# Turn, mix and projection of a node tile in one iteration of the chunk loop, with a written-out end for each convolution

## The chip, the cores and the metric

The kernel runs on one core of one Trainium2 chip. The metric is the device time of one execution in microseconds (us). Before the change it is 4954.78 us, the median of three runs (4953.78 to 4971.25).

## What is computed

A graph network on 12,500 nodes of 256 features and 200,000 edges sorted by destination. First `h = relu(layernorm(x))`, then two graph convolutions with self loops, then a projection, added to x:

```
h = h @ W_pre + b_pre
h = relu(gcn(h, W1, b1)); h = relu(gcn(h, W2, b2))
x = x + h @ W_post + b_post
gcn: out[d] = sum over edges (s, d) of (h @ W)[s] * dinv[s] * dinv[d]; out + b
```

Then a second layer: `h = relu(layernorm(x))`, `xt = h @ weight`, four attention heads whose logits come from the rows of the two ends of an edge, a softmax over the heads, and a weighted sum of the heads, which is added to x. Only the first n = 12,500 edges are used for it.

## The kernel before, in words

Nodes lie in 98 tiles (TILES) of 128 rows. Edges lie in 1568 chunks of 128, eight chunks to a half, two halves to an iteration, 98 iterations (ITERS) and 196 halves to a convolution. A convolution is c = 0 or c = 1.

**Gathers.** POOL (L631 to L637) issues one indirect DMA for each chunk: it fetches the table rows of the chunk's 128 sources into G. G has 12 portions (PORTIONS) of one half each, so before a half's first gather POOL waits until PE has finished the half 12 before it (`g_agg`, L635). The second convolution's first gather waits until the whole second table is in DRAM (`c1_w`, L630).

**Sums.** PE multiplies each chunk with a 0/1 selection matrix that DVE made (`chunk`, L959) and adds the eight products of a half in PSUM. Its last matmul signals `g_agg`. DVE adds the sum to one or two accumulator tiles (L1380), makes the selection for the half four later (`select`), and after an even half 2i makes the scaled rows of tile i-1 (`rows`, L1280, signal `c_tmp`). A matmul of f32 shows as two records in the profile: a chunk is x2.

**Work of a node tile, c = 0.** PE turns the rows (`turn`, L922), ACT copies them out (`lift`, L689), PE multiplies by Wc (`mix`, L931), ACT applies bias and relu (`relu_mixed`), PE multiplies by W2 (`project`, L942), ACT scales the result and writes it to `tsb` (`table_row`, L709), and SP stores it as a tile of the second table.

**Work of a node tile, c = 1.** `turn`, ACT's `relu_rows`, `project` by Wp; DVE's `residual` (L1291) adds x and takes mean and variance, with a square root on ACT in the middle; ACT's `normed` (L718) writes h; PE turns h (`turn_normed`, L949), ACT copies it (`normed_turned`), PE multiplies by Wx (`attention`, L954), ACT copies the result (`projected`, L730), and SP stores it to `xtab` and `ltab`. The attention stage, which follows, waits for all of these stores (L546, L613).

**The order.** Each engine runs its own list in order, written out by hand; waits for semaphores are the only tie. PE places the tile work between the chunks j = 0 to 15 of iteration i (L1000 to L1013). Before the change: for c = 0, `mix(i-3)` ahead of j = 2, `project(i-3)` ahead of j = 8, `turn(i-2)` ahead of j = 12; for c = 1, `turn_normed(i-4)` ahead of j = 2, `project(i-3)` ahead of j = 6, `attention(i-4)` ahead of j = 10, `turn(i-2)` ahead of j = 12. Four more passes of the loop without chunks finish the last tiles. ACT's list (L794 to L810) follows the same order. DVE runs `residual(i-3)` in iteration i (L1389 to L1393) and three residuals after the loop.

Of the kernel before, what the change touches and what calls it, by code (L numbers as in the profile page):

```python
# [29 lines left out]
CPH = CPG * HALF  # L30
# [15 lines left out]
def build_gnn(nc, x, src, dst, W_pre, b_pre, W1, b1, W2, b2, W_post, b_post, weight, attn_l,  # L46
# [5 lines left out]
    TILES = ceil(N, P)  # L52
    LAST = N - (TILES - 1) * P
    NP = TILES * P
    ITERS = ceil(E, CPI * P)
# [26 lines left out]
    with ExitStack() as ctx:  # L82
# [283 lines left out]
        def due(t):  # L366
            return 0 <= t < TILES
# [283 lines left out]
        def _(act):  # L651
            act.wait_ge(s_esrc, 16 * (1 + (FULL % P > 0) + (REST > 0)))
            act.copy(rawf_s, raw_s).then_inc(s_raws, 1)
            n = 0
# [34 lines left out]
            def lift(t):  # L689

                act.wait_ge(c_T, t + 3)
                act.copy(zc[:, :, :].rearrange("p k n -> p (k n)"), pT[0][:, 0:D])
                act.copy(sd_row, pT[0][0:1, D:D + P]).then_inc(c_l, 1)  # L693

            def relu_mixed(t):

                act.wait_ge(c_m, t + 1)
                act.wait_ge(c_a, t + 1)
                for m in range(KH):
                    ins = act.activation(z[:, m, :], pX[:, m * P:(m + 1) * P], ACT.Relu, bias=b1_c[:, m:m + 1])  # L700
                ins.then_inc(c_z, 1)
# [7 lines left out]
            def table_row(t):  # L709

                if isinstance(t, int):
                    act.wait_ge(c1_w[t % 2], 16 * (t // 2 + 1))
                else:
                    act.wait_ge(c1_w[0], t * 16 + 16)
                act.wait_ge(c_a, t + 2)
                act.activation(tsb[:, t % 2 if isinstance(t, int) else 0, :], pA[0][:, 0:D], ACT.Copy, scale=dinv[:, bass.ds(t, 1)]).then_inc(c_out, 1)
# [75 lines left out]
            bad = act.value_load(flag_i[0:1, 0:1], min_val=0, max_val=1)  # L792
            with act.If(bad == 0):
                for c in range(2):  # L794
                    for i in range(2, ITERS + 4):
                        if c == 0:
                            if due(i - 3):
                                relu_mixed(i - 3)
                                table_row(i - 3)
                            if due(i - 2):  # L800
                                lift(i - 2)
                        else:
                            if due(i - 4):
                                normed_turned(i - 4)
                            if due(i - 3):
                                normed(i - 3)
                            if due(i - 4):
                                projected(i - 4)
                            if due(i - 2):
                                relu_rows(i - 2)  # L810
                fast_attention()
            with act.Else():
                act.sem_inc(w_done, 1)
# [22 lines left out]
        def _(pe):  # L836
# [160 lines left out]
            with pe.If(bad == 0):  # L997
                for c in range(2):

                    for i in range(ITERS + 4):  # L1000
                        for j in range(CPI):
                            if j == 2 and c and due(i - 4):
                                turn_normed(i - 4)
                            if j == 2 and c == 0 and due(i - 3):
                                mix(i - 3)
                            if j == (6 if c else 8) and due(i - 3):
                                project(c, i - 3)
                            if j == 10 and c and due(i - 4):
                                attention(i - 4)
                            if j == 12 and due(i - 2):  # L1010
                                turn(c, i - 2, i % 2)
                            if i < ITERS:
                                chunk(c, 2 * i + j // CPH, j % CPH)  # L1013
                transpose_sel(0, 0, 0, True)
                for q in range(2):
                    pick(0, q, False)
                with pe.Fori(1, BATCHES // 2 - 1) as j:
                    for q in range(2):
                        pick(j, q, False)
                for q in range(2):  # L1020
                    pick(BATCHES // 2 - 1, q, True)
            with pe.Else():
                pe.wait_ge(s_din, 16)
                pe.transpose(pX[:, 0:TILES], degr, ident[0:TILES, 0:TILES]).then_inc(s_degT, 1)
                for c in range(2):
                    n = width(c)
# [17 lines left out]
        def _(dve):  # L1044
# [317 lines left out]
            with dve.If(bad == 0):  # L1362
                link(dve.tensor_copy(iota_p, iota[:, :]))
                link(dve.tensor_copy(bias_p, b2_bc[:, :]))
                for H in range(RING):
                    select(H)
                for c in range(2):
                    loaded, wide = 0, D if c else D + 1
                    for n in range(HALVES):
                        H = n + c * HALVES  # L1370
                        at = first_tile(n)
                        dve.wait_ge(g_agg, H + 1)
                        if H:
                            dve.wait_ge(g_add, 2 * H)
                        for a, mask in enumerate((here, beyond)):
                            T = at + a + c * TILES
                            if at + a >= loaded:
                                dve.wait_ge(a_in[T % AR], 16 * (T // AR + 1))
                                loaded += 1
                            dve.scalar_tensor_tensor(out=row(T, wide), in0=sums[H % SUMS][:, 0:wide],  # L1380
                                                     scalar=mask[:, n:n + 1], in1=row(T, wide),
                                                     op0=ALU.mult, op1=ALU.add).then_inc(g_add, 1)
                        if H + RING < 2 * HALVES:
                            select(H + RING)
                        if n % 2 == 0:
                            if due(n // 2 - 1) and n // 2 < TILES - 1:
                                dve.wait_ge(g_add, 2 * H + 2)
                                rows(c, n // 2 - 1, (n // 2 - 1) % 2, 1)
                            if c and due(n // 2 - 3):  # L1389
                                if n // 2 == 3:  # L1390
                                    for s in range(2):
                                        dve.wait_ge(c1_w[s], 16 * (TILES // 2 + 1))
                                residual(n // 2 - 3)  # L1393
                    dve.wait_ge(g_add, 2 * (c + 1) * HALVES)
                    for t in (TILES - 2, TILES - 1):
                        rows(c, t, t % 2, 1)
                    if c:
                        for t in range(TILES - 3, TILES):
                            residual(t)
                for q in range(2):  # L1400
                    select_f(q, q)
                dve.wait_ge(f_T, 2)
# [83 lines left out]
```

## Time and profile before

| | us |
|---|---|
| median of 3 runs | 4954.78 |
| profiled execution, its own time | 4990.98 |
| profiled execution, span | 4989.2 |
| first gather / last gather of c = 0 | 167.0 / 2399.6 |
| first gather / last gather of c = 1 | 2481.8 / 4712.5 |
| first gather of the attention stage | 4798.9 |

Busy shares of the span: PE 54%, POOL 62%, DVE 27%, ACT 9%. The mean granted clock of TensorE is 0.711 of full speed. The profile is one execution, 36.2 us longer than the median. In the timeline each row has its start, its length, engine, line, operation, output and inputs and, in brackets, how long the engine had been idle and what released it.

### The profile page before, as it was taken

How to read it: one execution, taken by the hardware profiler on the slowest of the kernel's cores; microseconds unless marked ns; L12 is line 12 of the kernel's file. 1: busy time of each engine (PE TensorE's matmuls, PEld its weight loads, DVE VectorE, ACT ScalarE, POOL GpSimd, SP SyncE). 2: the span in 40 equal slices, each digit the busy share in tenths (PEclk: the TensorE clock that was granted, in tenths of full speed). 3: DMA queues.
4: the chain of work that ended last, by engine and by line, in shares of the span. 5: the costliest groups of instructions: out<-in, count | busy, mean ns of one | idle time of the engine just before them, and what ended most of it. 6: DMA issues, size and time to landing. Idle time of an engine off the chain costs nothing.

```text
span 4989.2 us, 31799 instructions
## 1 busy us (share of the span) xinstructions
PE 2687.9 (54%) x10154; PEld 2099.1 (42%) x10154; DVE 1346.5 (27%) x2984; ACT 441.6 (9%) x1265; POOL 3096.6 (62%) x3240
## 2 busy tenths in 40 slices
PE   3325465555555655656634555555555555555675
PEld 2214344444444444445522444444434434444453
DVE  8201111112111211211202322332222323223357
ACT  2100000000000000000100000000000000000022
POOL 0566666666666666666275666666666666666535
PEclk5557776777777777767756777777777777777765
DMA  6433343433343433333133444444444444444336
GB/s 188 125 94 101 104 107 104 107 104 104 104 107 103 107 105 104 104 104 107 57 105 91 118 114 114 117 112 117 114 112 119 115 112 118 113 116 116 99 106 186
DMA packets 318169, 556.09 MB, mean 111 GB/s; under 512 B 79912, under 2 KB 217976, under 8 KB 318008
## 3 DMA queue, kind: packets, MB, share of 16 engines
q0 software_dynamic: 153184, 413.34, 31.4%
q1 hardware_dynamic: 164824, 140.76, 9.4%
q8 instruction: 82, 1.34, 0.1%
q14 instruction: 79, 0.65, 0.0%
HBM read 489.06 MB, written 64.78 MB: 111 GB/s over the span
## 4 chain that ended last, share of the span: by engine, by line
another core or an unknown queue 46%; issue 24%; PE 19%; DVE 6%; ACT 4%; DMA 1%; SPq 0%; POOL 0%; ACTq 0%; DVEq 0%; POOLq 0%
PE agg L968 7%; PE pD L968 4%; PE pA L846 2%; PE pX L938 2%; PE pX L939 2%; ACT xin L700 1%; DVE acc L1380 1%; PE pT L840 1%; DVE sel L1136 1%; DVE xin L1126 1%; DVE sel L1351 0%; ACT h L723 0%; ACT xin L707 0%; PE pA L994 0%
## 5 line engine op out<-in xcount | busy, mean ns | idle before, releaser
L608 POOL DMA_INDIRECT G<-tab,idx x3126 | 2970.1, 950 | 1734.9 <-issue 1069.7
L968 PE MATMUL agg<-G,sel 128*128 128x257 f32 (+1 forms) x4192 | 1253.0, 444 | 235.3 <-issue 203.9
L968 PEld LDWEIGHTS agg<-G,sel 128*128 128x128 f32 x4192 | 929.5, 228 | 428.5 <-issue 271.9
L1380 DVE SCALAR_TENSOR_TENSOR acc<-agg,here,acc 128x257 f32<-128x257 f32 (+1 forms) x262 | 127.0, 485 | 2353.9 <-remote 1879.7
L968 PE MATMUL pD<-G,sel 128*128 128x257 f32 (+1 forms) x2080 | 644.1, 455 | 85.0 <-issue 81.1
L968 PEld LDWEIGHTS pD<-G,sel 128*128 128x128 f32 x2080 | 475.3, 234 | 188.4 <-issue 104.8
L1276 DVE TENSOR_TENSOR sel<-rel,pA 128x1024 f32<-128x1024 f32 x392 | 474.5, 1211 | 0.0
L938 PE MATMUL pX<-xin,Wc 128*128 128x128 f32 x784 | 169.0, 349 | 488.1 <-ACT xin L693 402.2
L846 PE MATMUL pA<-W2s,xin 128*128 128x256 f32 x392 | 137.4, 484 | 416.0 <-ACT xin L700 212.9
L1380 DVE SCALAR_TENSOR_TENSOR acc<-pD,here,acc 128x257 f32<-128x257 f32 (+1 forms) x130 | 63.0, 485 | 1105.0 <-remote 818.4
L938 PEld LDWEIGHTS pX<-xin,Wc 128*128 128x128 f32 x784 | 132.5, 234 | 529.6 <-ACT xin L693 417.1
L846 PE MATMUL pX<-Wx,hT 128*128 128x264 f32 x392 | 140.4, 492 | 351.1 <-issue 258.1
L846 PEld LDWEIGHTS pA<-W2s,xin 128*128 128x128 f32 x392 | 90.3, 243 | 449.9 <-ACT xin L700 222.8
L846 PE MATMUL pA<-Wp,xin 128*128 128x256 f32 x392 | 144.5, 506 | 236.3 <-ACT xin L707 210.3
L846 PEld LDWEIGHTS pX<-Wx,hT 128*128 128x128 f32 x392 | 92.4, 245 | 380.3 <-issue 267.3
L840 PE MATMUL pT<-ident,h 128*128 128x128 f32 x196 | 55.6, 377 | 295.0 <-issue 246.5
L846 PEld LDWEIGHTS pA<-Wp,xin 128*128 128x128 f32 x392 | 97.1, 258 | 276.2 <-ACT xin L707 231.4
L608 POOL DMA_INDIRECT lg<-ltab,fst x98 | 118.6, 1210 | 133.5 <-DMA ltab<-xin 85.4
L840 PEld LDWEIGHTS pT<-ident,h 128*128 128x128 f32 x196 | 24.2, 173 | 337.1 <-issue 281.4
L700 ACT ACTIVATE xin<-pX,b_c 128x128 f32<-128x128 f32 x196 | 61.4, 364 | 886.4 <-remote 649.0
L1380 DVE SCALAR_TENSOR_TENSOR acc<-agg,beyond,acc 128x257 f32<-128x257 f32 (+1 forms) x262 | 124.8, 476 | 0.0
L939 PE MATMUL pX<-xin,bc_row 1*128 1x128 f32 x392 | 117.0, 386 | 0.0
(182 smaller groups left out, 1663.9 us busy)
## 6 DMA issues: line engine op xcount, KB each, us to landing
G<-tab,idx POOLq DMA_INDIRECT x3126
tab<-G SPq DMA_DIRECT2D x14, 910.0 KB, 5.1
acc<-tab SPq DMA_DIRECT2D x98, 130.0 KB
xtab<-xin SPq DMA_DIRECT2D x98, 130.0 KB
tab<-tsb SPq DMA_DIRECT2D x98, 128.0 KB
acc<-tab SPq DMA_DIRECT2D x98, 128.0 KB
xres<-acc SPq DMA_DIRECT2D x98, 128.0 KB
xin<-xres SPq DMA_DIRECT2D x14, 896.0 KB
```

The lines of the kernel that those rows point to most:

```text
L608: return pool.indirect_dma_start(out=to, out_offset=None, in_=table, in_offset=bass.IndirectOffsetOnAxis(ap=index, axis=0))
L700: ins = act.activation(z[:, m, :], pX[:, m * P:(m + 1) * P], ACT.Relu, bias=b1_c[:, m:m + 1])
L840: ins = pe.transpose(to[:, k * P:(k + 1) * P], of(k), ident[:, :])
L846: ins = pe.matmul(to[:, 0:n], lhsT(k), w[:, k, :], start=(k == 0), stop=(k == KH - 1))
L938: pe.matmul(to, Wc[:, k, m * P:(m + 1) * P], zc[:, k, :], start=(k == 0), stop=False)
L939: ins = pe.matmul(to, bc_row[0:1, m * P:(m + 1) * P], sd_row, start=False, stop=True)
L968: ins = pe.matmul(sums[H % SUMS][:, 0:n_c], sel[:, H % RING * CPH + j, :], G[:, H % PORTIONS * CPG + j, 0:n_c], start=(j == 0), stop=(j == ...
L1126: dve.tensor_tensor(ones_low[unit % BR][:, 0:n // 4, :, :], low_b[:, at:at + n].rearrange("p (q j) -> p q j", j=4).unsqueeze(2) .to_broadc ...
L1136: return dve.bn_stats(moms[:, m, :], xb[:, b % XB, m % FB, 0:D])
L1276: dve.tensor_tensor(sel[:, s * CPH:(s + 1) * CPH, :], rel[:, n * CPH:(n + 1) * CPH].unsqueeze(2).to_broadcast([P, CPH, P]), iota_p.unsquee ...
L1380: dve.scalar_tensor_tensor(out=row(T, wide), in0=sums[H % SUMS][:, 0:wide], scalar=mask[:, n:n + 1], in1=row(T, wide), op0=ALU.mult, op1=A ...
```

## The change

PE's loops keep all chunks in their order and place the work of a tile nearer together. For c = 0, `turn(i-2)` stands ahead of j = 2, `mix(i-2)` ahead of j = 6 and `project(i-2)` ahead of j = 10 of the same iteration. For c = 1, `turn(i-2)` stands ahead of j = 2, `attention(i-3)` ahead of j = 4, `project(i-2)` ahead of j = 6 and `turn_normed(i-2)` ahead of j = 15. The four passes without chunks are replaced by a written-out end for the last two tiles. ACT's and DVE's lists follow; a residual comes one iteration sooner. No instruction is added or taken away.

```diff
 ACT
-                    for i in range(2, ITERS + 4):
+                    for t in range(TILES - 2):
                         if c == 0:
-                            if due(i - 3): relu_mixed(i - 3); table_row(i - 3)
-                            if due(i - 2): lift(i - 2)
+                            lift(t)
+                            relu_mixed(t)
+                            table_row(t)
                         else:
-                            normed_turned(i - 4) / normed(i - 3) / projected(i - 4) / relu_rows(i - 2)
+                            relu_rows(t)
+                            if t:
+                                projected(t - 1)
+                            normed(t)
+                            normed_turned(t)
+                    if c == 0:
+                        lift(TILES - 2)
+                        relu_mixed(TILES - 2)
+                        lift(TILES - 1)
+                        table_row(TILES - 2)
+                        relu_mixed(TILES - 1)
+                        table_row(TILES - 1)
+                    else:
+                        relu_rows(TILES - 2)
+                        relu_rows(TILES - 1)
+                        projected(TILES - 3)
+                        for t in (TILES - 2, TILES - 1):
+                            normed(t)
+                            normed_turned(t)
+                            projected(t)
 PE
-                    for i in range(ITERS + 4):
+                    for i in range(ITERS):
                         for j in range(CPI):
-                            if j == 2 and c and due(i - 4):
-                                turn_normed(i - 4)
-                            if j == 2 and c == 0 and due(i - 3):
-                                mix(i - 3)
-                            if j == (6 if c else 8) and due(i - 3):
-                                project(c, i - 3)
-                            if j == 10 and c and due(i - 4):
-                                attention(i - 4)
-                            if j == 12 and due(i - 2):
+                            if j == 2 and due(i - 2):
                                 turn(c, i - 2, i % 2)
+                            if j == 4 and c and due(i - 3):
+                                attention(i - 3)
+                            if j == 6 and c == 0 and due(i - 2):
+                                mix(i - 2)
+                            if j == (6 if c else 10) and due(i - 2):
+                                project(c, i - 2)
+                            if j == 15 and c and due(i - 2):
+                                turn_normed(i - 2)
+                            chunk(c, 2 * i + j // CPH, j % CPH)
+                    if c == 0:
+                        turn(0, TILES - 2, TILES % 2)
+                        mix(TILES - 2)
+                        turn(0, TILES - 1, 1 - TILES % 2)
+                        project(0, TILES - 2)
+                        mix(TILES - 1)
+                        project(0, TILES - 1)
+                    else:
+                        for t in (TILES - 2, TILES - 1):
+                            turn(1, t, t % 2)
+                            project(1, t)
+                        attention(TILES - 3)
+                        for t in (TILES - 2, TILES - 1):
+                            turn_normed(t)
+                            attention(t)
 DVE
-                            if c and due(n // 2 - 3):
+                            if c and due(n // 2 - 2):
...
-                                residual(n // 2 - 3)
+                                residual(n // 2 - 2)
...
-                        for t in range(TILES - 3, TILES):
+                        for t in (TILES - 2, TILES - 1):
                             residual(t)
```

## Rows read from the trace of the kernel before

**Rows 1.** Instructions of line 608 (ns min/median/max, first and last start)
```profile
L608 POOL DMA_INDIRECT G<-tab,idx x3126: 943/949/1227, 167.0 to 4712.5; - x196
```

**Rows 2.** Windows view: busy us of PE, PEld, DVE, ACT, POOL; clock; DMA
```profile
346.80:2400.50 2053.70, 1163.27 (x4563) 925.57 (x4563) 383.71 (x630) 143.39 (x447) 1361.82 (x1435) 0.73 0.39 105
2661.60:4713.50 2051.90, 1121.00 (x3928) 874.30 (x3928) 614.64 (x1609) 155.33 (x445) 1365.20 (x1435) 0.73 0.43 115
```

**Rows 3.** Timeline, POOL and DVE (start, length, work, [idle before <- releaser])
```profile
346.81 0.95 POOL L608 DMA_INDIRECT G<-tab,idx  x1 [19.56 <-remote]
381.15 0.94 POOL L608 DMA_INDIRECT G<-tab,idx  x1 [4.49 <-remote]
...
3772.50 0.95 POOL L608 DMA_INDIRECT G<-tab,idx  x1 [4.67 <-remote]
3806.79 0.95 POOL L608 DMA_INDIRECT G<-tab,idx  x1 [4.54 <-remote]
...
3823.89 0.48 DVE L1380 SCALAR_TENSOR_TENSOR acc<-pD,here,acc 128x256 f32<-128x256 f32 x1 [9.73 <-remote]
```

**Rows 4.** Timeline after the second convolution's last gather: one cycle
```profile
4728.81 0.48 DVE L1380 SCALAR_TENSOR_TENSOR acc<-agg,here,acc 128x256 f32<-128x256 f32 x1 [5.49 <-PE agg L968]
...
4731.58 0.42 DVE L1299 TENSOR_TENSOR acc<-pA,tsb 128x256 f32<-128x256 f32 x1
...
4735.18 0.44 PE L840 MATMUL pT<-ident,h 128*128 128x128 f32 x2 [0.98 <-ACT h L723]
4735.45 1.89 PE L968 MATMUL agg<-G,sel 128*128 128x256 f32 x8
4737.18 1.03 PE L846 MATMUL pA<-Wp,xin 128*128 128x256 f32 x4
4738.05 1.89 PE L968 MATMUL agg<-G,sel 128*128 128x256 f32 x8
4739.11 0.48 DVE L1380 SCALAR_TENSOR_TENSOR acc<-agg,here,acc 128x256 f32<-128x256 f32 x1 [2.69 <-PE agg L968]
4739.77 1.05 PE L846 MATMUL pX<-Wx,hT 128*128 128x264 f32 x4
```

**Rows 5.** Timeline: PE after longer idle times
```profile
2403.35 2.07 PE L846 MATMUL pA<-W2s,xin 128*128 128x256 f32 x4 [2.65 <-ACT xin L700]
...
4715.72 0.48 DVE L1380 SCALAR_TENSOR_TENSOR acc<-pD,here,acc 128x256 f32<-128x256 f32 x1 [8.34 <-remote]
4722.08 0.69 PE L840 MATMUL pT<-ident,h 128*128 128x128 f32 x2 [4.37 <-ACT h L723]
```

**Rows 6.** Timeline: last even half and last chunks of the second convolution
```profile
4768.99 0.48 DVE L1380 SCALAR_TENSOR_TENSOR acc<-agg,here,acc 128x256 f32<-128x256 f32 x1 [3.82 <-PE agg L968]
...
4771.63 1.89 PE L968 MATMUL agg<-G,sel 128*128 128x256 f32 x8
```

**Rows 7.** Timeline: the second convolution's end
```profile
4791.98 0.44 PE L840 MATMUL pT<-ident,h 128*128 128x128 f32 x2 [2.27 <-ACT h L723]
4792.89 2.13 PE L846 MATMUL pX<-Wx,hT 128*128 128x264 f32 x4 [0.46 <-ACT hT L728]
4795.58 0.38 ACT L734 COPY xin<-pX 128x264 f32<-128x264 f32 x1 [2.75 <-DMA ltab<-xin]
```

**Rows 8.** Timeline: the first convolution's end
```profile
2459.22 1.90 PE L968 MATMUL agg<-G,sel 128*128 128x257 f32 x8
2463.08 0.61 DVE L1288 TENSOR_SCALAR xin<-acc,dinv 128x257 f32<-128x257 f32 x2
2464.72 0.27 PE L928 MATMUL pT<-ident,xin 128*1 128x128 f32 x1
2465.91 0.71 PE L938 MATMUL pX<-xin,Wc 128*128 128x128 f32 x4 [0.70 <-ACT xin L693]
2472.13 1.23 PE L938 MATMUL pX<-xin,Wc 128*128 128x128 f32 x4 [0.61 <-ACT xin L693]
2478.84 0.47 ACT L716 ACTIVATE tsb<-pA,dinv 128x256 f32<-128x256 f32 x1 [2.23 <-PE pA L846]
```

More of the change, by code:

```diff
@@ L794, in _ @@
                 for c in range(2):
-                    for i in range(2, ITERS + 4):
+                    for t in range(TILES - 2):
                         if c == 0:
[L797 to L801, printed above, removed]
-                        else:
[L803 to L810, printed above, removed]
+                            lift(t)
+                            relu_mixed(t)
+                            table_row(t)
+                        else:
+                            relu_rows(t)
[18 more added lines that the diff above has]
+                            projected(t)
                 fast_attention()
@@ L998, in _ @@
                 for c in range(2):
-                    for i in range(ITERS + 4):
+                    for i in range(ITERS):
                         for j in range(CPI):
-                            if j == 2 and c and due(i - 4):
-                                turn_normed(i - 4)
-                            if j == 2 and c == 0 and due(i - 3):
-                                mix(i - 3)
-                            if j == (6 if c else 8) and due(i - 3):
-                                project(c, i - 3)
-                            if j == 10 and c and due(i - 4):
-                                attention(i - 4)
-                            if j == 12 and due(i - 2):
-                                turn(c, i - 2, i % 2)
-                            if i < ITERS:
-                                chunk(c, 2 * i + j // CPH, j % CPH)
+                            if j == 2 and due(i - 2):
+                                turn(c, i - 2, i % 2)
+                            if j == 4 and c and due(i - 3):
[22 more added lines that the diff above has]
+                            attention(t)
                 transpose_sel(0, 0, 0, True)
@@ L1388, in _ @@
                                 rows(c, n // 2 - 1, (n // 2 - 1) % 2, 1)
-                            if c and due(n // 2 - 3):
-                                if n // 2 == 3:
+                            if c and due(n // 2 - 2):
+                                if n // 2 == 2:
                                     for s in range(2):
                                         dve.wait_ge(c1_w[s], 16 * (TILES // 2 + 1))
-                                residual(n // 2 - 3)
+                                residual(n // 2 - 2)
                     dve.wait_ge(g_add, 2 * (c + 1) * HALVES)
```

## The prediction, on record before the change was run

> **What bounds the kernel now.** I first looked at the two convolutions, which fill the time from 167.0 to 4712.5 us [rows 1]: 3126 gathers by POOL, one for each chunk. The windows [rows 2] cut out each convolution from POOL's first pause to its last gather. The reader is to see that the two are alike: 1435 gathers in 2053.7 us and 1435 in 2051.9 us, 1.431 us each, although PE's list for an iteration has 51 records of matmuls in the first (32 for chunks, turn 3, mix 12, project 4) and 44 in the second (32, 2, 4, 2, 4), in another order. POOL's own timeline [rows 3] shows of what 1.431 us is made. While POOL isn't held, a gather takes 0.95 us and 0.30 us of issue, 1.25 in all. Then it is held. From 346.81 to 381.15 and from 3772.50 to 3806.79 lie 34.34 and 34.29 us: 24 gathers at 1.25 (30.1 us), with a pause of 4.5 us at the end, counted from the last gather. The first pause of the kernel, 19.56 us, came after the 128 gathers issued from 167.0 on (179.8 us). So 24 gathers cost 4.2 us of waiting beyond the usual 0.3, and 128 cost 19.3: about 0.145 us for each gather and 0.7 for each pause. The pause grows with what POOL has issued, in both convolutions by the same law. The nominal reason is `g_agg`, that PE is twelve halves behind. But PE is busy for only 1163 and 1121 of some 2050 us, and the longer list has no longer pauses. I can't say what holds the signals back; I take from the rows that the order of the tile work isn't what sets it.
>
> That leaves two places where POOL has nothing more to issue and PE's list sets the end: from 2400.5 to the second convolution's start, and from 4713.5 to the attention stage. There PE still has twelve halves to add and the last tiles to finish.
>
> **Steady part, both convolutions.** No matmul, copy or DMA is added; each iteration has the same ones. I cost it at nothing. What hides it is the 22.9 us that POOL takes for an iteration's 16 gathers (16 x 1.431) against 10.3 us in which PE gets through one when nothing holds it [rows 4]. SP's queue gets each residual's store, the next load of x and the two stores of `projected` about an iteration sooner, and all loads of accumulators stand behind them in the same order; nothing there is late today. The DVE wait for `c1_w`, moved from tile 0's old place to one iteration sooner, has behind it only DVE work of a convolution whose gathers already waited for the same stores. If the cover is gone, the price is in the rivals.
>
> **First convolution's end.** Within the loop the order costs nothing: four chunks lie between `turn`, `mix` and `project`, 1.72 us (4738.05 to 4739.77) [rows 4], and ACT's lift has done its work 1.2 us after the turn (2464.72 to 2465.91) [rows 8]. Each iteration keeps its PE work, so the last chunks still end at 2460.9 (2459.22 and 1.7). DVE's rows for the last two tiles start at 2463.08 and the first is there at 2463.4. Before, `mix(95)` and `project(95)` stood in between and the turn of tile 96 came at 2464.7; now it can come at 2463.5. Then: mix(96) 1.2 us later, 2464.7; its relu as before 2.8 us after (before: 2465.91, next PE step at 2468.8), so turn(97) at 2467.6; project(96) behind it, 0.4 and 1.4 us, to 2469.5; then mix(97), which started at 2472.13. From there to the last table row was 6.7 us (2472.13 to 2478.84), all of it still needed. It ends 2.6 us sooner; I take -2.5. Bounds: 0, if the idle PE falls to the lower clock at the first turn, and -5.5, if it keeps the full clock to the end (the last 6.7 us would then be some 4).
>
> **Second convolution, the twelve halves after the last gather.** Here the order costs. Take the cycle that begins with DVE's addition of an even half at 4728.81 [rows 4]. Rows, residual and `normed` follow; PE turns h at 4735.18, 6.37 us after. This chain has the same links after the change, but it now belongs to the turn that stands ahead of j = 15 of the same iteration, where it stood ahead of j = 2 of the next. Ahead of it PE has only chunks 8 to 14, 7 x 0.43 = 3.0 us, where it had eight chunks, `attention`, `turn` and two more. It waits some 3.6 us in each iteration where it waited 0.98. Queued behind it on PE: chunk 15, with it `g_agg` of the odd half, and all of the next iteration. After the turn of h (0.27) come chunk 15, 0 and 1 (1.29), turn (0.22), two chunks (0.86), attention (0.89), two chunks, project (0.87), two chunks (0.86 each pair), and 0.2 us until DVE sees it: 6.3 us. The cycle becomes 6.37 + 6.3 = 12.7 where it is 10.3 (4728.81 to 4739.11): +2.4. Six even halves are left after the last gather, the first at 4715.72 [rows 5] and the last at 4768.99 [rows 6]: five cycles, +12.0. After the last one the chain lacks the selection (1.2 us), h comes at 5.2, and with the turn and chunk 15 the end comes at 5.9 us; it came at 4.4 (4768.99 to 4773.4): +1.5. Together +13.5.
>
> To this comes the clock. After 2.65 us idle PE's next four records took 2.07 us [rows 5], after 0.98 us idle four took 1.03 (at 4737.18) [rows 4]: the lower and the full level of its clock, 1.2 and 2.4 GHz. From the turn at 4722.08, which had 4.37 us idle ahead of it, to the next even half it took 6.73 us, and 3.93 in the cycle of rows 4: 2.8 more. A wait of 3.6 us lies between; I take 1.5 us for each of four cycles (the first has its 4.37 us idle already), 6.0 in all. Bounds: 0, if the clock holds, and 4 x 2.8 = 11.2. So this part costs +19.5 (13.5 to 24.7). A gain is excluded: h can't be there before its own rows are.
>
> By the Trainium skill (TensorE: Matmul & The Clock Gate, HAM oscillation) a loop whose every tile has such a wait can start every tile at the low clock; by this rule the sum would take the upper bound, 5.2 us more than mine. The trace agrees for single idle times of 2.65 and 4.37 us, but has no loop with one of 3.6 us in each turn.
>
> **Second convolution's end.** Before, the last `projected` started at 4795.58 [rows 7], 22.2 us after the last chunk (4773.4). Now from the last chunk: DVE's additions and rows 1.6, turn, relu and projection of tile 96 to 3.9; the residual's last part and h as in 4731.58 to 4735.18, 3.6 us, and 1.5 for ACT, which must first take attention(95), issued behind both projections: h turned at 9.0; hT and attention (4791.98 to 4792.89 is 0.9, then 2.3): 12.3 with its copy; ACT's square root for tile 97 stands behind that copy, h 2.0 later; turned at 14.7, attention at 15.6, the copy at 17.9. -4.3. Bounds: -2, if all of it runs at the low clock, and -6. What is late next is the same: the stores to `ltab`, as today.
>
> **Sum.** -2.5 + 19.5 - 4.3 = +12.7 us on the profiled execution, 4989.2 to 5001.9 of span. The median of the runs is 36.2 below the profiled execution's own time of 4990.98; I carry the difference over: 4954.8 + 12.7 = 4967. From the bounds, +2 (13.5 - 5.5 - 6) to +23 (24.7 - 0 - 2): 4957 to 4978.
>
> **Rivals.**
> A, the wait goes into POOL's pauses (slower). If in the second convolution a pause ends only when an odd half is done, and the even half before it became visible in the same moment, the chain of 6.37 us lies inside the pause. Halves come by three, so every second of the 60 pauses (2052 / 34.3) ends at an odd half: 30 x 6.4 = +191 at most; if half of them are hit, 4955 + 96 + 13 = 5064. It decides from the point where the even half isn't seen before POOL stops. For it: a long time lies between PE's last matmuls of a half and DVE's sight of them. Against it: with POOL resumed at 3806.79 and stopped 30.1 us later, the even half was seen at 3823.89, 13 us before the stop [rows 3].
> B, fewer pauses (faster). With mix and project in one iteration PE may get further before signals stall. A pause's fixed part is 0.7 us; there are 60 in each convolution if all come after three halves: at most -84, and half of it, with the sum above, gives 4955 - 42 + 13 = 4926. For it: 19.3 us once for 128 gathers is cheaper than 4.2 for each 24. Against it: 1.431 in both orders.
> C, the cycle isn't stretched, since PE is slowed anyway, and only the ends count: -6.8, 4948. Against it: in that stretch PE waits 0.98 us in 10.3 [rows 4], so whatever is added shows.
> D, the ends too are hidden, and the wait too: 4955.
>
> **Chances.** The forecast 0.50, C and D 0.20 together, A 0.13, B 0.10; the rest, 0.07, is unknown and split over both sides. The comparison can tell about 0.5%, 25 us. The forecast, C and D lie within it, but for 0.03 of the forecast's upper side. So: faster 0.12, same 0.69, slower 0.19. The range takes in C and parts of A and B: 4936 to 5010. The forecast's own is 4957 to 4978.
>
> **What would show it.** In the profile after: 1.43 us for each gather in both convolutions; in the second, after the last gather, a PE row of turned h with 3 to 4 us idle ahead of it in each cycle and 12.7 to 15.5 us from one even half to the next; 0.5 to 2.5 us less idle at the turn of tile 96 in the first; some 18 us from last chunk to last `projected`. I am wrong if the pauses change their law, or if PE doesn't wait for h there.

## The result, and the profile after

Twelve timed runs of the changed kernel gave 4977.24 us (4970.6 to 4981.18); twelve of the kernel before, on the same chip, gave 4956.51. The ratio is 1.004 (95% interval 1.003 to 1.0049), so the change costs about 20 us (15 to 24). One of the twelve executions of the kernel before took 10226.58 us; it counts as slow and is left out of the ratio. The forecast was +12.7 (+2 to +23 by its own bounds), too little to tell, by way of a new wait for h after the last gather. The wait came, and the time lies within those bounds, near the upper one; +12.7 itself lies below the measured interval.

The profiled execution took 4981.05 us (span 4979.2). The one before [rows 1 to 8] took 4990.98 and is 34 us above what that kernel takes beside this one (before_again, below, shows why), so the two spans can't be subtracted. What can be compared is a stretch in which PE's list alone sets the time. That is the one after POOL's last gather: 4712.54 to 4798.9 before, 86.4 us; now 4686.85 to 4790.20, 103.3 us. It grew by 16.9.

The timeline of the kernel after shows this stretch. The columns are start, length, engine, line, operation, tiles and, in brackets, the idle time before it and what ended it; L1404, L850, L856 and L978 are before's L1380, L840, L846 and L968. The DVE rows are the even halves, the PE rows the turned h (all but one at 4766.78, after the last even half):

```profile
4684.34 0.95 POOL L608 DMA_INDIRECT G<-tab,idx  x1 [4.04 <-remote]
...
4690.47 0.48 DVE L1404 SCALAR_TENSOR_TENSOR acc<-pD,here,acc 128x256 f32<-128x256 f32 x1 [4.35 <-PE pD L978]
...
4696.82 0.69 PE L850 MATMUL pT<-ident,h 128*128 128x128 f32 x2 [3.37 <-ACT h L723]
...
4705.98 0.48 DVE L1404 SCALAR_TENSOR_TENSOR acc<-agg,here,acc 128x256 f32<-128x256 f32 x1 [5.58 <-PE agg L978]
...
4712.34 0.44 PE L850 MATMUL pT<-ident,h 128*128 128x128 f32 x2 [3.37 <-ACT h L723]
...
4713.24 1.91 PE L978 MATMUL agg<-G,sel 128*128 128x256 f32 x4
...
4720.36 0.48 DVE L1404 SCALAR_TENSOR_TENSOR acc<-agg,here,acc 128x256 f32<-128x256 f32 x1 [4.88 <-PE agg L978]
...
4726.72 0.69 PE L850 MATMUL pT<-ident,h 128*128 128x128 f32 x2 [3.37 <-ACT h L723]
...
4734.61 0.48 DVE L1404 SCALAR_TENSOR_TENSOR acc<-pD,here,acc 128x256 f32<-128x256 f32 x1 [4.30 <-PE pD L978]
...
4740.96 0.69 PE L850 MATMUL pT<-ident,h 128*128 128x128 f32 x2 [3.37 <-ACT h L723]
...
4750.24 0.48 DVE L1404 SCALAR_TENSOR_TENSOR acc<-agg,here,acc 128x256 f32<-128x256 f32 x1 [5.70 <-PE agg L978]
...
4755.60 0.44 PE L850 MATMUL pT<-ident,h 128*128 128x128 f32 x2 [2.37 <-ACT h L723]
...
4761.94 0.48 DVE L1404 SCALAR_TENSOR_TENSOR acc<-agg,here,acc 128x256 f32<-128x256 f32 x1 [4.55 <-PE agg L978]
...
4767.05 0.60 PE L978 MATMUL agg<-G,sel 128*128 128x256 f32 x2
```

The cycles are 15.51, 14.38, 14.25, 15.63 and 11.70 us, 71.47 together, against 53.27 before (4715.72 to 4768.99) [rows 5, 6]. In the first four PE stands idle for 3.37 us ahead of the turned h, where it stood 0.98 [rows 4]; in the fifth, whose chain has no selection in it, for 2.37. At three of the four the turn itself takes 0.69 us for two records, where it took 0.44: PE has fallen to the lower clock level (granted clock 0.50 from 4696.82 to 4702.0). At the other, 4712.34, the turn takes 0.44 and PE is low right behind it: four records of chunks take 1.91 us there instead of 1.03. In the fifth cycle PE keeps the full clock (1.00 from 4755.60 to 4761.0). The chain from the even half to the turned h is 6.35 us (4690.47 to 4696.82), as before (6.37).

The end of the second convolution, after the last chunk, in the same columns:

```profile
4772.25 2.07 PE L856 MATMUL pA<-Wp,xin 128*128 128x256 f32 x4 [0.47 <-ACT xin L707]
...
4775.35 0.38 ACT L734 COPY xin<-pX 128x264 f32<-128x264 f32 x1 [3.15 <-PE pX L856]
4775.62 0.21 ACT L721 ACTIVATE rs<-rs 128x1 f32<-128x1 f32 x1
...
4777.68 0.69 PE L850 MATMUL pT<-ident,h 128*128 128x128 f32 x2 [2.42 <-ACT h L723]
...
4781.04 0.38 ACT L734 COPY xin<-pX 128x264 f32<-128x264 f32 x1 [2.27 <-PE pX L856]
4781.32 0.21 ACT L721 ACTIVATE rs<-rs 128x1 f32<-128x1 f32 x1
...
4783.38 0.69 PE L850 MATMUL pT<-ident,h 128*128 128x128 f32 x2 [2.42 <-ACT h L723]
...
4786.74 0.38 ACT L734 COPY xin<-pX 128x264 f32<-128x264 f32 x1 [2.27 <-PE pX L856]
```

The first row is the projection of tile 97, at the lower clock level. Each square root (L721) stands behind a copy (L734) on ACT. From the last chunk (4767.65) to the last copy are 19.1 us; it was 22.2 [rows 7].

The end of the first convolution, from its last turn but one:

```profile
2449.39 0.27 PE L938 MATMUL pT<-ident,xin 128*1 128x128 f32 x1 [2.37 <-DVE xin L1312]
...
2450.49 1.22 PE L948 MATMUL pX<-xin,Wc 128*128 128x128 f32 x4 [0.61 <-ACT xin L693]
...
2457.41 1.06 PE L948 MATMUL pX<-xin,Wc 128*128 128x128 f32 x4
...
2463.95 0.47 ACT L716 ACTIVATE tsb<-pA,dinv 128x256 f32<-128x256 f32 x1 [2.22 <-PE pA L856]
```

`mix(96)` takes 1.22 us for four records where it took 0.71 at the full clock [rows 8], and PE stays low. From the last chunk (2446.9) to the last table row are 17.1 us; it was 17.9 (2460.9 to 2478.84).

### The profile page after: what moved, and what is told of

Read it like the earlier page. It is cut to its first block, busy times and chain, and to the rows that moved or that the text cites. A ratio compares the mean times of both kernels' runs of the same rounds, so it can differ in the third digit from the quotient of the medians.

```text
span 4979.2 us, 31799 instructions
## 1 busy us (share of the span) xinstructions
PE 2731.3 (55%) x10154; PEld 2154.8 (43%) x10154; DVE 1349.2 (27%) x2984; ACT 459.9 (9%) x1265; POOL 3090.4 (62%) x3240
## 3 DMA queue, kind: packets, MB, share of 16 engines
q8 instruction: 82, 1.34, 0.1%
## 4 chain that ended last, share of the span: by engine, by line
another core or an unknown queue 48%; issue 20%; PE 19%; DVE 9%; ACT 3%; DMA 1%; SPq 1%; POOL 0%; DVEq 0%; ACTq 0%; POOLq 0%
PE agg L978 7%; PE pA L856 4%; PE pD L978 3%; DVE acc L1404 2%; PE pX L948 1%; PE pX L856 1%; PE pX L949 1%; ACT xin L700 1%; PE pT L850 1%; ACT tsb L716 1%; DVE sel L1160 1%; DVE xin L1309 1%; DVE stats L1325 1%; DVE acc L1323 1%
## 5 line engine op out<-in xcount | busy, mean ns | idle before, releaser
L978 PE MATMUL agg<-G,sel 128*128 128x257 f32 (+1 forms) x4192 | 1272.5, 453 | 91.9 <-issue 61.3
L978 PEld LDWEIGHTS agg<-G,sel 128*128 128x128 f32 x4192 | 957.1, 235 | 268.9 <-issue 98.0
L1404 DVE SCALAR_TENSOR_TENSOR acc<-agg,here,acc 128x257 f32<-128x257 f32 (+1 forms) x262 | 127.0, 485 | 2182.3 <-remote 1518.0
L978 PE MATMUL pD<-G,sel 128*128 128x257 f32 (+1 forms) x2080 | 633.5, 448 | 18.8 <-issue 14.9
L978 PEld LDWEIGHTS pD<-G,sel 128*128 128x128 f32 x2080 | 469.0, 232 | 106.0 <-issue 24.0
L850 PE MATMUL pT<-ident,h 128*128 128x128 f32 x196 | 64.0, 427 | 651.8 <-ACT h L723 331.1
L1404 DVE SCALAR_TENSOR_TENSOR acc<-pD,here,acc 128x257 f32<-128x257 f32 (+1 forms) x130 | 63.0, 485 | 1265.6 <-remote 1030.0
L856 PE MATMUL pA<-W2s,xin 128*128 128x256 f32 x392 | 170.4, 580 | 368.5 <-ACT xin L700 217.0
L850 PEld LDWEIGHTS pT<-ident,h 128*128 128x128 f32 x196 | 27.0, 194 | 691.4 <-ACT h L723 347.1
L856 PEld LDWEIGHTS pA<-W2s,xin 128*128 128x128 f32 x392 | 104.5, 287 | 420.9 <-ACT xin L700 239.9
L856 PE MATMUL pA<-Wp,xin 128*128 128x256 f32 x392 | 139.4, 491 | 261.0 <-issue 194.6
L856 PEld LDWEIGHTS pA<-Wp,xin 128*128 128x128 f32 x392 | 94.8, 250 | 288.5 <-issue 201.0
L856 PE MATMUL pX<-Wx,hT 128*128 128x264 f32 x392 | 136.1, 480 | 102.1 <-ACT hT L728 99.9
L856 PEld LDWEIGHTS pX<-Wx,hT 128*128 128x128 f32 x392 | 91.8, 243 | 135.2 <-ACT hT L728 112.4
L1404 DVE SCALAR_TENSOR_TENSOR acc<-agg,beyond,acc 128x257 f32<-128x257 f32 (+1 forms) x262 | 124.6, 475 | 0.0
```

What stands on the lines that cost most here:

```text
L850: ins = pe.transpose(to[:, k * P:(k + 1) * P], of(k), ident[:, :])
L856: ins = pe.matmul(to[:, 0:n], lhsT(k), w[:, k, :], start=(k == 0), stop=(k == KH - 1))
L978: ins = pe.matmul(sums[H % SUMS][:, 0:n_c], sel[:, H % RING * CPH + j, :], G[:, H % PORTIONS * CPG + j, 0:n_c], start=(j == 0), stop=(j == ...
```

## The experiments

"First" and "last" are the starts of a convolution's first and last gather. The pauses are POOL's idle time ahead of a gather beyond the usual 0.3 us. All are read from POOL's timeline of the one profiled execution of each kernel; medians come from all its runs on that chip. A to D name the places where kernels ran side by side. A, B and C are three chips; D bears A's number, though the kernel before was 29 us shorter there, and whether it is the same chip at another time can't be told.

| kernel | chip | median / before there | c=0 first to last | to c=1's first | c=1 first to last | to attention | pauses c=0 / c=1 |
|---|---|---|---|---|---|---|---|
| before [rows 1] | – | 4954.8 | 2232.6 | 82.2 | 2230.8 | 86.4 | 274 / 269 |
| after | – | 4977.2 / 4956.5 | 2218.5 | 81.5 | 2220.0 | 103.3 | 261 / 263 |
| before_again | A | 4987.3 | 2232.8 | 75.6 | 2229.8 | 86.1 | 275 / 267 |
| first_only | A | 4994.0 / 4987.3 | 2248.9 | 78.0 | 2229.5 | 81.4 | 292 / 268 |
| second_only | A | 5005.5 / 4987.3 | 2233.2 | 80.9 | 2228.6 | 102.9 | 280 / 275 |
| h_next_j6 | A | 4992.8 / 4987.3 | 2239.7 | 85.0 | 2233.8 | 72.8 | 283 / 277 |
| after_again | B | 5034.8 / 4985.2 | 2241.7 | 81.5 | 2228.5 | 101.9 | 285 / 272 |
| mix_twice | B | 5019.0 / 4985.2 | 2247.6 | 95.8 | 2232.2 | 80.6 | 296 / 279 |
| depth6 | B | 4926.4 / 4985.2 | 2233.9 | 53.2 | 2230.1 | 53.9 | 281 / 276 |
| h_next_j6_second | B | 4989.3 / 4985.2 | 2235.4 | 72.7 | 2247.7 | 74.2 | 283 / 296 |
| depth3 | C | 4329.9 / 4330.0 | 1953.2 | 33.5 | 1955.2 | 34.7 | 0 / 0 |
| after_depth6 | C | 4328.3 / 4330.0 | 1953.1 | 31.2 | 1955.5 | 36.8 | 0 / 0 |
| depth6_j6 | C | 4326.8 / 4330.0 | 1953.3 | 31.3 | 1955.2 | 28.8 | 0 / 0 |
| depth3_again | D | 4870.2 / 4958.6 | 2218.6 | 36.7 | 2222.1 | 35.1 | 265 / 270 |

The stretch between the convolutions, where the code is before's at full depth, came out at 82.2, 75.6, 80.9 and 72.7: one execution reads it to some 10 us. The stretch to attention, where it is before's at full depth, was 80.6 to 86.4.

**before_again**: the kernel before, once more.

> The unchanged kernel once more, for a second profile. Theory: the earlier profiled execution of it (span 4989.2 us) was a slow draw for its gathers; a second one has a span of 4950 to 4970 us, with POOL's last gathers 10 to 15 us earlier in each convolution, and the same 61 us in each from the last gather to the last chunk. Rival: the new order itself shortened the steady part by some 14 and 11 us; then the second profile shows 2399.6 and 4712.5 us for the last gathers again.

4983.14 us, not the 4950 to 4970 that was expected, and nearly the same as the first profile stretch by stretch but for the one between the convolutions (75.6 against 82.2). All runs of this kernel at A lie near 4987 (4979.84 to 4991.63). So the 36 us between the profile and the median shown before are not the draw of one execution: they belong to the chip, or to its condition at the time. The rival, that the new order itself shortened the gathers by some 14 and 11 us, doesn't hold at A, where the new order's are 2248.9 and 2228.6 (first_only, second_only) against 2232.8 and 2229.8. This is why comparisons stay within a letter.

**first_only and second_only**: the new lists for one convolution, before's for the other.

```diff
 for c in range(2):
+    if c == 0:      # second_only: c == 1
+        ... loop and written-out end of the kernel after
+    else:
+        ... loop of the kernel before
```

> The new order and end for c = 0 alone; c = 1 as before. Theory: only the first convolution's end moves, -1 us (the changed kernel's trace has 17.1 us from last chunk to last table row, before had 17.9): same as before within 3 us. Rival (fewer or shorter pauses of POOL in the first convolution): 10 to 20 us faster than before. Rival (the new order lengthens them): over 5 us slower.

Ratio 1.0015 (1.0006 to 1.0024), +7 us (3 to 12): of what was expected, the rival that the new order lengthens the pauses. In the profile the first convolution's gathers took 2248.9 us against 2232.8. Its runs spread over 15 us (4987.44 to 5002.39), those of the kernel before over 12, so one profile doesn't give the size.

> The new order and end for c = 1 alone; c = 0 as before. Theory: the wait for h after the last gather (+19.8 us in the changed kernel's trace) less the shorter end (-3.0): 15 to 20 us slower than before, the whole of the change's cost. Rival (the cost lies in the first convolution or in both steady parts): under 8 us slower.

Ratio 1.0036 (1.0022 to 1.0049), +18 us. The stretch to attention grew by 16.8 (102.9 against 86.1), the gathers' didn't (2228.6 against 2229.8). Its six turns of h have 3.39, 3.38, 3.38, 3.38, 2.38 and 1.85 us idle ahead of them, as in the kernel after. So nearly all of the second half's cost is the wait for h after the last gather, and rival A, which puts it into POOL's pauses, gets no more than the 8 us by which the pauses grew, which don't show in the stretch. The two halves' +7 and +18 make 25 us, beside 20 (15 to 24) for the whole change, measured elsewhere.

**h_next_j6**: as after, but h is turned in the next iteration, with more chunks between. ACT's copy of the turned h moves with it, and the written-out end begins with tile 95's turn.

```diff
-                            if j == 4 and c and due(i - 3):
-                                attention(i - 3)
...
-                            if j == 15 and c and due(i - 2):
-                                turn_normed(i - 2)
+                            if j == 6 and c and due(i - 3):
+                                turn_normed(i - 3)
+                            if j == 10 and c and due(i - 3):
+                                attention(i - 3)
```

> As the changed kernel, but the turn of h goes ahead of j = 6 and attention ahead of j = 10 of the next iteration; both written-out ends kept (the turn of tile 95's h comes first there). Theory: PE no longer waits for h, an iteration after the last gather takes 9.2 us (before 10.3, changed 14.5); against the changed kernel -25 us, against before -5 to -12. Rival (the cost isn't that wait): within 8 us of the changed kernel, so still 12 us or more above before.

The timeline of DVE and PE after its last gather, even halves and the turned h:

```profile
4737.61 0.48 DVE L1406 SCALAR_TENSOR_TENSOR acc<-agg,here,acc 128x256 f32<-128x256 f32 x1 [1.28 <-PE agg L979]
...
4745.42 0.38 PE L851 MATMUL pT<-ident,h 128*128 128x128 f32 x2
...
4746.71 0.48 DVE L1406 SCALAR_TENSOR_TENSOR acc<-agg,here,acc 128x256 f32<-128x256 f32 x1 [1.50 <-PE agg L979]
...
4755.81 0.48 DVE L1406 SCALAR_TENSOR_TENSOR acc<-pD,here,acc 128x256 f32<-128x256 f32 x1 [1.50 <-PE pD L979]
```

PE no longer waits for h, and a cycle is 9.1 us (4737.61 to 4746.71), against 14.3 in after and 10.3 in before. The stretch to attention falls to 72.8 us, 30 less than second_only's 102.9. That is the counter-proof for the cause: moving two calls takes the whole end loss away and more. The total misses what was expected (5 to 12 us faster than before): it is 1.0015 (1.0006 to 1.0024), +5.5 us. In the profile what the end gained (13.3) was lost again in gathers (6.9 and 4.0) and in the first end (9.4, in the spread of that stretch).

**after_again**: the kernel after, on a chip where before's runs are beside it.

> The changed kernel once more, beside runs of the kernel before on the same chip. Theory: 15 to 30 us slower than before; in its profile some 20 us of it from the last gather to the last chunk of c = 1, and 0 to 15 us in POOL's pauses of c = 0, which were longer in the profile of the kernel with the new order for c = 0 alone (291.6 us against 274.9). Rival (that was chance): pauses of c = 0 within 4 us of 275.

Ratio 1.0111 (1.0095 to 1.0126), +50 us: more than twice what the first chip gave, and beyond the 15 to 30 expected. Its profiled execution is the shortest of its six, 5011.9 (the longest was 5046.7), 27 us over before's median: 16 of them at the end of c=1 (101.9 against some 86) and 7 in c=0's gathers (2241.7 against 2233.9 and 2235.4 of unchanged lists on B). Of what the longer executions lost, up to 35 us more, no trace exists; it stays open.

**mix_twice**: the kernel before, with twice the matmuls of `mix`, the second pair repeating the first.

```diff
-                for m in range(KH):
+                for m in (0, 1, 0, 1):
```

> The kernel before with each mix made twice (12 more PE records in an iteration of c = 0, 2.1 us at the full clock; the second writes the same values). Theory (the pauses follow the gathers that POOL has issued, not PE's work): first to last gather of c = 0 stays within 10 us of 2233; after the last gather 6 x 2.1 and two more mixes at the end, some 17 us more: +15 to +25 in all. Rival (PE's progress sets the pauses): 98 x 2.1, +150 to +200 us. Rival between: PE's records count in the slow stretches, +40 to +100.

Ratio 1.0071 (1.0056 to 1.0086), +34 us, for 15 to 25 expected. The windows view from 346.8 to 2382 us (length, then busy us and instructions of PE, PEld, DVE, ACT, POOL, then the clock) of h_next_j6_second, whose first convolution is before's on the same chip, and of mix_twice:

```profile
346.80:2382.00 2035.20, 1157.82 (x4503) 922.42 (x4504) 380.15 (x623) 142.49 (x444) 1342.94 (x1421) 0.73 0.38 105
```
```profile
346.80:2382.00 2035.20, 1320.65 (x5524) 1047.60 (x5525) 378.18 (x620) 141.71 (x440) 1333.18 (x1411) 0.79 0.38 104
```

PE has 163 us more to do and POOL makes 10 gathers fewer, which are 14 us. PE's work goes into its idle time but for a tenth; it sets the length of the pauses no further than that. It does set their place: 85 of the 92 pauses in c = 0 come after 16 gathers, where before_again has 37 after 16 and 34 after 24. The gathers took 12 to 14 us more than the unchanged ones on B (2247.6 against 2235.4 and 2233.9), over the 10 that were expected at most. The end, where only PE's list counts, grew by 14 to 23 (95.8 against 82.2 to 72.7 of unchanged lists).

**depth6**: the kernel before, with POOL held after 6 halves instead of 12. `g_agg` then says that PE has finished the half six before.

```diff
-                        if H >= PORTIONS:
-                            pool.wait_ge(g_agg, H - PORTIONS + 1)
+                        if H >= 6:
+                            pool.wait_ge(g_agg, H - 6 + 1)
```

> The kernel before, but POOL waits for the half 6 before its own instead of 12. Theory (the pauses follow POOL's issues, whatever the run-ahead): pauses sum to the same, and after the last gather of each convolution PE has six halves fewer to add, 6 x 5.1 us each: 50 to 62 us faster. Rival (the run-ahead hides PE's slow stretches): more or longer pauses, the steady part longer by at least what the ends give back, same or slower.

Ratio 0.9881 (0.9865 to 0.9896), −59 us, as expected. The gathers took as long as ever (2233.9 and 2230.1), the two ends 53.2 and 53.9. A run-ahead of 12 halves doesn't shorten the steady part: it only leaves PE twelve halves of work once POOL is done.

**h_next_j6_second**: c=0 as before, c=1 as in h_next_j6.

> c = 0 as before; c = 1 with the turn of h ahead of j = 6 and attention ahead of j = 10 of the next iteration and the written-out end. Theory: the end of c = 1 is 13 us shorter (72.8 us from last gather to the attention stage against 86, as the profile of the kernel with both had it), pauses of c = 1 up to 5 us longer: 6 to 13 us faster than before. Rival (c = 1 pays it back in its pauses): within 3 us of before.

Ratio 1.001 (1.0 to 1.0019), +4, where 6 to 13 us less than before were expected: the rival, that c = 1 pays it back, came. The end gained again (74.2, for 80.6 in mix_twice and some 86 at A), but the second convolution's gathers took 2247.7 us, where mix_twice and depth6, which leave it alone, have 2232.2 and 2230.1 on the same chip: +16, with pauses of 296 against 279 and 276. h_next_j6, with the same list in c = 1, had +4.0 there. The gain and the loss cancel but for a few us, as the total says.

**depth3, after_depth6, depth6_j6**: `3` for `6` in the kernel before; after and h_next_j6_second with depth 6.

> The kernel before, but POOL waits for the half 3 before its own. Theory (with 6 instead of 12 the steady part kept its length, 2233.9 and 2230.1 us, and each end lost some 30): three more halves fewer at each end, another 25 to 31 us, 85 to 95 us faster than before in all. Rival (with three halves of run-ahead, as many as a pause covers, POOL begins to wait beyond its pauses): slower than with 6, so less than 59 us faster, the steady part over 10 us longer.

> The changed kernel with POOL's wait for the half 6 before its own. Theory (the wait for h costs some 4 us for each even half that PE has left after the last gather): three even halves fewer, so its excess over the kernel before with 6, 4926 us, is 8 to 12 us less than the excess of the changed kernel over before at 12 (+50 on this chip, +21 on another); from last gather to last chunk of c = 1 some 10 us more than there instead of 20. Rival (the excess lies in POOL's pauses alone): the same excess as at 12.

> Candidate for the best: c = 0 as before, c = 1 with the turn of h ahead of j = 6 and attention ahead of j = 10 and the written-out end, POOL's wait for the half 6 before its own. Theory: the end of c = 1 is some 8 us shorter than with 6 alone (53.9 us from last gather to the attention stage become 46), pauses of c = 1 up to 15 us longer: between 4920 and 4935 us, no clear gain over 6 alone. Rival (the end counts in full, the longer pauses were chance): 4915 to 4920.

They ran on a chip where the kernel before takes 4330.04 us. Ratios: 0.9999 (0.999 to 1.0008), 0.9997 (0.9988 to 1.0006), 0.9992 (0.9983 to 1.0001). The expectations had assumed pauses, and there are none in these three, so of those expectations nothing was tested. This is the line of all gathers on the page of depth3 (busy, mean ns, idle ahead of it), which has 1734.9 us of idle time in the kernel before's own page:

```profile
L608 POOL DMA_INDIRECT G<-tab,idx x3126 | 2958.7, 946 | 1142.6 <-issue 1135.9
```

Of the 1142.6 us, 1135.9 are issue: the 0.30 ahead of each gather and the kernel's start. A gather comes each 1.25 us (1953.2 for 1563), and even a depth of 3 never holds POOL. Where it doesn't bind, the depth is worth nothing. depth6_j6 shows the better order once more: 28.8 us to attention, against 36.8 with the order of after. Neither shows in the total: 4326.8 and 4328.3 us against 4330.0.

**depth3_again**: the same kernel as depth3, on a chip with pauses.

> The kernel before with POOL's wait for the half 3 before its own, once more: its first runs fell on a chip where the kernel before takes 4330 us and POOL has no pauses, so a shorter run-ahead had nothing to give back (ratio 0.9999). Theory: on a chip with pauses (before at 4955 to 4987 us) it is 85 to 95 us faster than before; on one without, the same as before again. Rival (three halves are too few to cover a pause): on a chip with pauses less than the 59 us that 6 gave.

Ratio 0.9818 (0.9804 to 0.9831), −88 us. POOL's timeline, a pause late in the second convolution and the first gather of the attention stage:

```profile
4573.49 0.94 POOL L608 DMA_INDIRECT G<-tab,idx  x1 [4.48 <-remote]
...
4679.47 0.94 POOL L608 DMA_INDIRECT lg<-ltab,fst  x1 [34.17 <-DMA ltab<-xin]
```

The ends are 36.7 and 35.1 us, and the pauses of c = 1 stay at 4.5 after 24 gathers (62 of its 65). This version beats both kernels by 1.8% where there are pauses, and does no harm where there are none.

## Why the prediction was right, and where it was off

**The c=1 halves after the last gather: right.** Forecast +19.5. Measured from the last gather to the end of the last chunk: 80.8 us (4686.85 to 4767.65) against 60.9 (4712.54 to 4773.4), +19.9. The parts agree too: five cycles +18.2 (18.0 forecast as 12.0 and 6.0), the last half and the first one +1.7 (1.5).

**The clock in it: right in sum, but not cycle by cycle.** From the turned h to the next even half the forecast had 6.3 us at the full clock, 2.8 more in the first cycle as before, and 1.5 more in each of the four others: 8.8. Beyond 6.3 the five took 2.9, 1.7, 1.6, 3.0 and 0.0 us (the first 4696.82 to 4705.98, the last 4755.60 to 4761.94): 9.2. So two cycles paid the upper bound, two about the middle value and one nothing. The Trainium skill (TensorE: Matmul & The Clock Gate, HAM oscillation) has every tile of such a loop start cold. The trace agrees for the first four cycles: three turns of h are at the lower level (0.69 us) and the fourth falls right behind its turn. It doesn't for the fifth, which had 2.37 us idle ahead of it. And PE came back to the full level within each cycle, so that the price was the upper bound only twice.

**The c=1 end: right in direction, gain 1.2 too large.** −3.1 (19.1 against 22.2) for −4.3. The forecast had tile 96's h turned 9.0 us after the last chunk; it was 10.0 (4767.65 to 4777.68). ACT's square root stood behind the copy of attention(95), as the prediction had it, but that came late: ahead of it on PE the projection of tile 97 took 2.07 us (4772.25) at the lower clock level, where four such records take 1.03 at the full one. From there on only the turn itself (0.69 for 0.44) was dearer. second_only has the same 19.1.

**The c=0 end: mis-sized, and its gain not shown.** −0.8 (17.1 against 17.9) for −2.5. In this profile the reason is the one that its own bound names, idle PE falling to the lower clock: 1.22 us a group of `mix` instead of 0.71. But the clock decides more here than the order. From the last chunk's modelled end to the last table row before's list took 17.7 us in the first profile, 14.0 in before_again, 14.9 in second_only and 14.9 in h_next_j6_second; the new one took 16.9 in after, 14.4 in first_only, 14.4 in h_next_j6 and 16.9 in after_again. The two ranges overlap almost wholly.

**The steady part at nothing: not contradicted beside the first runs, off at A and B.** The ends add up to 19.9 − 3.1 − 0.8 = +16.0, which lies within the measured 15 to 24. The kernel before has no profile beside after's, but depth3_again ran where it takes 4958.6 us, and has gathers of 2218.6 and 2222.1; after's are 2218.5 and 2220.0. That speaks for an unchanged steady part there, and doesn't prove it. At A first_only puts +7 on the first convolution; its profiled gathers took 16 us longer at unchanged work. At B, in after_again, some 30 us of the +50 have no place in the ends. The prediction read "the order of the tile work isn't what sets it" from two convolutions that differ in order and agree in 1.431. A reordering within one lengthened its gathers by 16 us twice (first_only's c=0, h_next_j6_second's c=1), by 4 to 8 us three times (both of h_next_j6, after_again's c=0), and twice not at all (c=1 of second_only and of after_again). Three of these are the same list in c=0 and two the same in c=1, so a single profile gives no size. Unchanged lists agree to 5 us on one chip. So placement moves it, by a mechanism that no run here isolates.

**The law of the pauses: misread.** The prediction took "24 gathers and a pause of 4.5 us" for both convolutions. That holds for c = 1 before the change, where 58 of 60 pauses come after 24 gathers. In c = 0 there are 71 pauses, 39 after 24 gathers and 30, shorter ones, after 16. In the kernel after c = 1 has 78: 38 after 24 gathers, 26 after 16, 13 after 8. So one of the two signs of being wrong came in part: the order does change where the pauses fall. Their sum changes little, 260 to 296 us in every convolution with pauses, and the forecast needed no more than that.

**Rivals.** A: refuted in its size. second_only's pauses in c=1 rose by 8 us, not 96, and its stretch of gathers not at all. B: no reordered convolution had shorter gathers than the unchanged ones at the same place by more than 3.7 us (after_again's c=1, 2228.5 against 2232.2 and 2230.1), which is within their spread. Its price for a pause was too high too: second_only's c=1 has 20 pauses more than before_again's for those 8 us, 0.4 each and not 0.7. C: refuted by the 3.37 us of idle time in four of the five cycles. D: refuted by the +16.8 of second_only's stretch to attention.

**Open.** What makes the pauses. Their sum stays at 260 to 296 us in every profiled convolution but those of chip C, where there are none, and neither PE's work (mix_twice) nor the run-ahead (depth6, depth3_again) moves it by more than some 15 us. The trace does show what comes late. These are rows of all engines ahead of one pause of the kernel before:

```profile
985.20 0.48 PE L939 MATMUL pX<-xin,bc_row 1*128 1x128 f32 x2
985.62 2.87 PE L968 MATMUL pD<-G,sel 128*128 128x257 f32 x12
...
1004.83 0.63 ACT L700 ACTIVATE xin<-pX,b_c 128x128 f32<-128x128 f32 x2 [21.38 <-issue]
1005.51 2.07 PE L846 MATMUL pA<-W2s,xin 128*128 128x256 f32 x4 [17.03 <-issue]
...
1011.21 0.48 DVE L1380 SCALAR_TENSOR_TENSOR acc<-pD,here,acc 128x257 f32<-128x257 f32 x1 [22.01 <-remote]
...
1011.44 0.95 POOL L608 DMA_INDIRECT G<-tab,idx  x1 [4.49 <-remote]
```

PE had finished ACT's input by 985.7 and the half by 988.5, but ACT began 19 us and DVE 23 us later, and PE itself stood for 17 of them. ACT, DVE and PE stand still together, and POOL is the last to be held. In the same stretch of c = 0 (1000 to 2100 us) PE's longest wait is 22.3 us in the kernel before and 6.1 in depth3 on chip C. Why PE's results are taken up so late stays open. The Trainium skill (Runtime: NRT & Kernel Launch, Instruction fetch mechanics) says that each engine's sequencer fetches its instructions by a DMA queue of its own while it executes, and calls the cost mostly hidden; the pages of the kernels before and after, and of depth3 on chip C, have 82 packets of 1.34 MB on that queue, and no run here shows whether they come late. The kernel after at full depth wasn't run on chip C, so it isn't known whether it loses there too.

## What to carry to other kernels

Ask of every wait how long the chain behind it is, and place the waiting step that far back: with a chain of 6.4 us PE didn't wait when 14 chunks of 0.43 us and other work lay between, waited 1 us with ten, and 3.4 us with seven, which also cost it the full clock for a part of most cycles. A producer's run-ahead that doesn't shorten the steady part is paid back whole at the end of each stage, so measure a smaller depth first: two numbers in one wait were worth 88 us here, four times what the reordering moved. Time a change beside its base, and on more than one chip: the same two kernels differed by 20 us in one place and by 50 in another.

## What the runs showed of the hardware

The kernel before took 4330 us on chip C and 4955 to 4987 everywhere else. Taking depth3 on C in its place, the profile of before_again (4983.1) is 654 us longer: 542 are pauses, 42 and 51 the ends (75.6 and 86.1 against 33.5 and 34.7), and 12 the gathers themselves (2970.6 against 2958.7 busy us), 647 together. A gather's own time goes with the program, not with the chip: 946 ns for depth3 on C and D, 948 for the kernel after in both its profiles, 950 for the kernel before in both. PE's idle time of 3.37 us was followed by the lower clock level in all four cycles that had it, at once or right behind the turn. One of 2.37 us kept the full level in the fifth cycle, between chunks back to back, and one of 2.37 to 2.42 us stood beside the lower level at both convolutions' ends, where PE had other idle times around it (0.61 us at 2450.49, 1.49 and 0.47 ahead of 4772.25). Between 400 and 2100 us PE's longest idle time was 16.0 to 22.4 us in seven profiles with pauses (before, before_again, after, first_only, mix_twice, depth6, depth3_again), and no more than 6.1 in depth3 and after_depth6 on C.
